# State-space stage: separate homes for delta times x, a first convolution on VectorE, and Softplus in one ScalarE operation

## What is computed

```python
xc, z = jnp.split(layernorm(x) @ W_in.T, 2, axis=-1)
xc = jax.nn.silu(causal_depthwise_conv(xc, conv_w) + conv_b)      # 4 taps per channel
dBC = xc @ W_x.T                                                  # rank 64, then B and C of 16 each
delta = jax.nn.softplus(dBC[..., :64] @ W_dt.T + b_dt)            # the step size
deltaA = jnp.exp(delta[..., None] * -jnp.exp(A_log))
BX = delta[..., None] * Bm[:, :, None, :] * xc[..., None]
hs = scan(h = deltaA * h + BX)                                    # along the 512 positions
y = jnp.einsum('bldn,bln->bld', hs, Cm) + Dp * xc
x = x + (y * jax.nn.silu(z)) @ W_out.T
```

## Time and profile before

| | us |
|---|---|
| median of 3 runs (range) | 2030.31 (2026.47 to 2031.36) |
| the profiled execution's own time | 2027.92 |
| its span, first to last instruction | 2026.2 |
| first scan (half 0 of batch 0) starts | 87.77 |
| state-space block ends, about | 993 |

### The profile page before, as it was taken

How to read it: one execution, slowest core, us unless ns; L and a number is a source line. 1 busy time by engine, 2 the same in 40 slices (tenths; PEclk the granted TensorE clock), 3 DMA queues, 4 the chain that set the end, 5 groups by cost and what they waited for, 6 DMA issues and landing times. The chain is left out here.

```text
span 2026.2 us, 34133 instructions
## 1 busy us (share of the span) xinstructions
PE 1317.7 (65%) x14100; PEld 627.8 (31%) x14100; DVE 1335.6 (66%) x1625; ACT 914.5 (45%) x1685; POOL 1075.5 (53%) x463
## 2 busy tenths in 40 slices
PE   6175765758485765843488746577767777556876
PEld 3021322223131322220233323244444445443333
DVE  1388889998988889899650023786678658617002
ACT  4267475666657475654222214454445434113220
POOL 0488999989898999989600011331452245312000
PEclk9587777869686877866698877787778877678988
DMA  3725537282726547280399950113211222219997
GB/s 93 176 52 148 134 96 185 54 200 53 188 69 154 128 104 167 54 201 28 104 403 421 421 200 14 45 39 67 65 41 46 65 65 44 65 35 389 406 421 282
DMA packets 193707, 300.07 MB, mean 148 GB/s; under 512 B 82704, under 2 KB 125200, under 8 KB 177168
## 3 DMA queue, kind: packets, MB, share of 16 engines
q1 hardware_dynamic: 188512, 295.17, 48.5%
q10 hardware_dynamic: 4688, 2.19, 0.4%
q0 software_dynamic: 352, 0.52, 0.1%
HBM read 255.37 MB, written 42.47 MB: 147 GB/s over the span
## 5 line engine op out<-in xcount | busy, mean ns | idle before, releaser
L369 POOL TENSOR_TENSOR state<-dx_rep,b_rep 128x2048 f32<-128x2048 f32 x128 | 579.0, 4530 | 25.0 <-PE psum L739 24.9
L597 DVE TENSOR_TENSOR_SCAN psum<-psum,state 128x1024 f32<-128x1024 f32 x160 | 365.1, 2282 | 57.3 <-POOL state L369 33.8
L482 ACT ACTIVATE psum<-delta_rep,a_neg 128x511 f32<-128x511 f32 x512 | 331.4, 684 | 68.8 <-DVE state L597 68.7
L739 PE MATMUL psum<-state,sel 128*32 128x512 f32 x1024 | 182.1, 808 | 210.3 <-POOL state L378 209.9
L597 DVE TENSOR_TENSOR_SCAN state<-psum,state 128x1024 f32<-128x1024 f32 x96 | 218.8, 2279 | 37.4 <-ACT psum L482 37.4
L378 POOL TENSOR_TENSOR state<-state,c_rep 128x1024 f32<-128x1024 f32 x96 | 226.4, 2361 | 0.0
L663 PE MATMUL psum<-xt,w_in 128*128 128x512 f32 x256 | 142.7, 709 | 101.2 <-ACT z_silu L441 47.9
L604 DVE TENSOR_TENSOR state<-psum,c_rep 128x1024 f32<-128x1024 f32 x160 | 195.9, 1224 | 5.5
L479 ACT COPY psum<-zeros 128x2 f32<-128x2 f32 x160 | 26.2, 164 | 249.4 <-DVE state L604 241.7
L739 PEld LDWEIGHTS psum<-state,sel 128*32 128x32 f32 x1024 | 27.8, 127 | 334.1 <-issue 314.9
L1852 PE MATMUL psum<-xt_delta,w_qkv 128*128 128x512 f32 x192 | 110.5, 717 | 12.1 <-DVE attn_t L1666 11.3
(11 more groups left out here) (219 smaller groups left out, 2477.4 us busy)
## 6 DMA issues: line engine op xcount, KB each, us to landing
moe_w_set<-in_w SPq DMA_DIRECT2D x30, 4096.0 KB, 33.2
delta_rep<-delta_scratch SPq DMA_DIRECT2D x128, 256.0 KB, 4.7
dx_rep<-dx_scratch SPq DMA_DIRECT2D x128, 256.0 KB, 7.6
b_rep<-bc_scratch SPq DMA_DIRECT2D x32, 256.0 KB, 4.8
delta_scratch<-delta SPq DMA_DIRECT2D x32, 256.0 KB, 5.3
dx_scratch<-delta SPq DMA_DIRECT2D x32, 256.0 KB, 2.0
c_rep<-bc_scratch SPq DMA_DIRECT2D x32, 256.0 KB, 8.1
moe_x<-x_after SPq DMA_DIRECT2D x16, 512.0 KB, 8.8
```

The lines of the kernel that those rows point to most:

```text
L369: nc.gpsimd.tensor_tensor(ring[q % RING][:, :, :], dx_rep[u % CHUNKS][:, :, :], free_bcast(b_rep[q // QPB % 2][:, g, :], 1, CB), ALU.mult) ...
L482: ins = nc.scalar.activation(dec[:, i, 1:], delta_rep[u % CHUNKS][:, c, 1:], ACT.Exp, scale=a_neg[:, dt * CB + c, g:g + 1])
L597: nc.vector.tensor_tensor_scan(bx if by_pool(k) else flat, flat, bx, 0.0, ALU.mult, ALU.add).then_inc(S["scan_done"], 1)
L739: ins = nc.tensor.matmul(bank[32 * c:32 * c + 32, :], sel[:, :], ring[q % RING][:, c, :], start=False, stop=(g == NG4 - 1), skip_group_che ...
```

## The change

- **Softplus.** The four ACT operations and the DVE sum of a block become one `ACT.Softplus` from PSUM into `delta`, which raises `delta_ready` itself. Softplus is in a table set of its own; after each pair of blocks the program asks for the Exp and Ln set again.
- **Homes for dx.** `delta_x` writes elsewhere: for batch 0 into the second `z_silu` buffer, later for blocks 0, 1 into `x_res` and for 2, 3 into `xt`. It no longer waits for the store of delta, but (later batches) for `x_stored` or for `z_psum`; ACT's `xt_copies` now waits for `d_stored` of blocks 2, 3.
- **First convolution.** For batch 0, ACT copies the projection into `xpad` and scales the same PSUM bank by the last tap with the bias; DVE adds the other three taps (three `scalar_tensor_tensor` per block), and ACT's Silu follows. The matmuls and their wait for `conv_diag` go; the making of `conv_diag` (16 operations, L614) moves behind the taps, `dp_diag` and `a_neg`.
- **SP's order for batch 0.** Block by block: store delta, store dx, load the chunk (blocks 0, 1).

```diff
+        def dx_home(b, t):
+            if b == 0:
+                return zs[1][:, t, :]
+            return x_res[:, 2 * t:2 * t + 2, :].rearrange("p s d -> p (s d)") if t < 2 else xt[:, t - 2, :]
...
-                for pair in ((0, 1), (2, 3)):
-                    for t in pair:
-                        store_delta(0, t)
-                    for t in pair:
-                        store_dx(0, t)
-                        if t < 2:
-                            load_chunk(0, t)
-                        if t == 0:
-                            load_replicated(0, 1)
+                for t in range(DT):
+                    store_delta(0, t)
+                    store_dx(0, t)
+                    if t < 2:
+                        load_chunk(0, t)
+                    if t == 0:
+                        load_replicated(0, 1)
...
-                    pool.wait_ge(S[f"d_stored{t}"], 32 * b + 16)
-                    nc.gpsimd.tensor_tensor(delta[:, t, :], delta[:, t, :], xc[b % 2][:, t, :], ALU.mult).then_inc(
+                    if b >= 2 and t < 2:
+                        pool.wait_ge(S["x_stored"], 16 * (b - 1))
+                    if b and t >= 2:
+                        pool.wait_ge(S["z_psum"], DT * (b + 1))
+                    nc.gpsimd.tensor_tensor(dx_home(b, t), delta[:, t, :], xc[b % 2][:, t, :], ALU.mult).then_inc(
...
+                        if b >= 2:
+                            act.wait_ge(S[f"d_stored{2 + kt}"], 32 * b)
                         act.wait_ge(S["xt_psum"], KD * b + kt + 1)
...
+                def first_tap(t):
+                    act.wait_ge(S["xp_psum"], t + 1)
+                    if t >= 2:
+                        act.wait_ge(S["first_conv"], t - 1)
+                    bank = xbank(0, t)
+                    nc.scalar.copy(xpad[t % 2][:, KC - 1:], bank[:, :])
+                    nc.scalar.activation(bank[:, :], bank[:, :], ACT.Identity, bias=conv_b[:, t:t + 1],
+                                         scale=conv_w[:, t, KC - 1:KC]).then_inc(S["xp_read"], 1)
...
-                def softplus_parts(b, pair):
+                def step_sizes(b, pair):
                     for t in pair:
                         act.wait_ge(S["delta_psum"], DT * b + t + 1)
                         if b:
                             act.wait_ge(S[f"d_stored{t}"], 32 * b)
...
+                        nc.scalar.activation(delta[:, t, :], dbank(b, t)[:, :], ACT.Softplus,
+                                             bias=b_dt[:, t:t + 1]).then_inc(S["delta_ready"], 1)
+                    nc.scalar.preload_act_table_set("natural_log_exp_and_others")
...
+                for t in range(DT):
+                    first_tap(t)
                 for t in range(DT):
                     first_silu(t)
-                    if t < 2:
-                        xpad_copy(0, t + 2)
-                nc.scalar.preload_act_table_set("natural_log_exp_and_others")
                 copy_dbc(0)
                 act.wait_ge(S["proj_loaded"], 16 * 3)
-                for t in range(DT):
-                    softplus_parts(0, (t,))
+                step_sizes(0, range(DT))
...
-                def softplus_sum(b, t):
+                def first_taps(t):
+                    for k in range(KC - 1):
+                        if k == 0:
+                            dve.wait_ge(S["xp_read"], t + 1)
+                        else:
+                            dve.wait_ge(S["conv_step"], 2 * t + k)
+                        bank = xbank(0, t)[:, :]
+                        nc.vector.scalar_tensor_tensor(bank if k < KC - 2 else xc[0][:, t, :], xpad[t % 2][:, k:k + L],
+                                                       conv_w[:, t, k:k + 1], bank, ALU.mult, ALU.add).then_inc(
+                            S["conv_step"] if k < KC - 2 else S["first_conv"], 1)
...
-                for t in range(DT):
-                    convolve(0, t)
```

More of the change, by code:

```diff
@@ L223, in mamba_phase @@
             "ln_stats", "ln_mv", "ln_var", "ln_rstd", "ln_shift", "ln_done", "xt_psum", "xt_ready", "xp_psum", "xp_read",
-            "conv_diag", "conv_psum", "conv_done", "xc_ready", "z_psum", "z_read", "dbc_psum", "dbc_ready", "bc_stored",
-            "b_loaded0", "b_loaded1", "c_loaded0", "c_loaded1", "delta_psum", "soft_abs", "soft_exp", "soft_ln", "delta_ready", "dx_ready",
+            "conv_diag", "conv_psum", "conv_done", "conv_step", "first_conv", "xc_ready", "z_psum", "z_read", "dbc_psum", "dbc_ready", "bc_stored",
+            "b_loaded0", "b_loaded1", "c_loaded0", "c_loaded1", "delta_psum", "delta_ready", "dx_ready",
             "d_stored0", "d_stored1", "d_stored2", "d_stored3", "delta_loaded0", "delta_loaded1", "delta_loaded2",
@@ L278, in store_dx @@
                     sp.wait_ge(S["dx_ready"], DT * b + t + 1)
-                    sp.dma_start(dx_dram[b, t * P:(t + 1) * P, :], delta[:, t, :]).then_inc(S[f"d_stored{t}"], 16)
+                    sp.dma_start(dx_dram[b, t * P:(t + 1) * P, :], dx_home(b, t)).then_inc(S[f"d_stored{t}"], 16)
                 def load_chunk(b, t):
@@ L421, in xpad_copy @@
                     if t >= 2:
-                        act.wait_ge(S["conv_psum"], DT * b + t - 1)
+                        act.wait_ge(S["conv_psum"], DT * (b - 1) + t - 1)
                     nc.scalar.copy(xpad[t % 2][:, KC - 1:], xbank(b, t)[:, :]).then_inc(S["xp_read"], 1)
                 def conv_copy(b, t):
-                    act.wait_ge(S["conv_psum"], DT * b + t + 1)
+                    act.wait_ge(S["conv_psum"], DT * (b - 1) + t + 1)
                     nc.scalar.activation(xc[b % 2][:, t, :], xbank(b, t)[:, :], ACT.Identity,
                                          bias=conv_b[:, t:t + 1]).then_inc(S["conv_done"], 1)
+                def first_tap(t):
[6 more added lines that the diff above has]
+                                         scale=conv_w[:, t, KC - 1:KC]).then_inc(S["xp_read"], 1)
                 def first_silu(t):
-                    act.wait_ge(S["conv_psum"], t + 1)
-                    nc.scalar.activation(xc[0][:, t, :], xbank(0, t)[:, :], ACT.Silu, bias=conv_b[:, t:t + 1]).then_inc(
-                        S["xc_ready"], 1)
+                    act.wait_ge(S["first_conv"], t + 1)
+                    nc.scalar.activation(xc[0][:, t, :], xc[0][:, t, :], ACT.Silu).then_inc(S["xc_ready"], 1)
                 def conv_silu(b):
@@ L453, in softplus_parts @@
                             act.wait_ge(S[f"d_stored{t}"], 32 * b)
-                        nc.scalar.activation(delta[:, t, :], dbank(b, t)[:, :], ACT.Relu, bias=b_dt[:, t:t + 1])
-                        nc.scalar.activation(dbank(b, t)[:, :], dbank(b, t)[:, :], ACT.Abs,
-                                             bias=b_dt[:, t:t + 1]).then_inc(S["soft_abs"], 1)
-                    for t in pair:
-                        act.wait_ge(S["soft_abs"], DT * b + t + 1)
-                        nc.scalar.activation(dbank(b, t)[:, :], dbank(b, t)[:, :], ACT.Exp,
-                                             scale=-1.0).then_inc(S["soft_exp"], 1)
-                    for t in pair:
-                        act.wait_ge(S["soft_exp"], DT * b + t + 1)
-                        nc.scalar.activation(dbank(b, t)[:, :], dbank(b, t)[:, :], ACT.Ln,
-                                             bias=1.0).then_inc(S["soft_ln"], 1)
+                        nc.scalar.activation(delta[:, t, :], dbank(b, t)[:, :], ACT.Softplus,
+                                             bias=b_dt[:, t:t + 1]).then_inc(S["delta_ready"], 1)
+                    nc.scalar.preload_act_table_set("natural_log_exp_and_others")
                 def half_decay(k):
@@ L546, in _ @@
                         if i == 22:
[L547 removed]
+                            step_sizes(n, (0, 1))
                         if i == 25:
[L549 removed]
+                            step_sizes(n, (2, 3))
                         if i == 29:
@@ L610, in _ @@
                                         ALU.add).then_inc(S["sel_ready"], 1)
+                dve.wait_ge(S["pads_zero"], 3)
                 dve.wait_ge(S["conv_loaded"], 16 * 2)
+                for t in range(DT):
+                    first_taps(t)
+                dve.wait_ge(S["params_loaded"], 16 * N_PARAMS)
+                for t in range(DT):
+                    nc.vector.tensor_scalar(dp_diag[:, t, :], ident[:, :], dp[:, t:t + 1], None,
+                                            ALU.mult).then_inc(S["dp_diag"], 1)
+                dve.wait_ge(S["a_exp"], NJ)
+                nc.vector.tensor_scalar(a_neg[:, :, :], a_neg[:, :, :], -1.0, None, ALU.mult).then_inc(S["a_ready"], 1)
                 for t in range(DT):
```

25 lines of the change are left out of this document (2 added, 23 removed).

## The result

| | before | after |
|---|---|---|
| median, us (range) | 2030.31 (2026.47 to 2031.36) | 1964.91 (1959.82 to 1966.89) |
| profiled execution, us (its span) | 2027.92 (2026.2) | 1966.89 (1965.2) |

The ratio is 0.9678, with a 95% interval of 0.9651 to 0.9706. 1974 was forecast, with a range of 1956 to 1999. The profiled span fell by 61.0 us.

What follows compares the result with a forecast made beforehand. It took the start's chain and, in the loop, DVE's own work plus late ACT as the bound. Start 30.5 plus loop 26 gave 56.5 us off 2027.92, 1971.4, plus 2.4 for the median: 1974, range 1956 to 1999.

Steps and rivals of the forecast that it cites:

- What bounds the loop: State-space loop: DVE's own work plus places where ACT is late, 60.8 us of DVE waits over 30 waits.
- POOL's waits are slack: Loop: POOL's 42.4 us of waits for delta's stores cost nothing, unless they come back through PE.
- The paragraph on quad 0: Next batch's first quad: POOL starts 3.7 us earlier, DVE 4; late chunks could cost 1 us a batch, 7 in all.
- Start, convolution: Batch 0: taps of 0.75 us from 18.4, cold projection 5.2 from 26.3, `dbc` at 32.1 against 39.91; 1.8 worse at 1.2 GHz.
- Start, chunk: Batch 0, from `dbc` to first scan: chunk 0 called at 41.9, first scan at 57.2 instead of 87.77, gaining 30.5 us.
- Loop, step sizes: End of each batch: half 26 2.4 us earlier, a removed sum 1.2, a shorter wait 0.3; 3.9 a batch, 27 in seven.
- Loop, the norm's shift: DVE's `norm_shift`, now meeting `delta_x` on POOL, would cost up to 0.3 us in six batches.
- the forecast's own case: Whole kernel: start and loop gains as worked out, 1974 us, with its own range 1966 to 1992; chance 0.71.
- All 42.4 us of GpSimd's waits back: Rival, loop: POOL's waits were on the path through PE, so 73 us gained in total, 1957 us; chance 0.12.
- A drain behind each load: Rival, ACT in the loop: each table switch costs 2.57 us, loop gains 0.2 a batch, total 1998 us; chance 0.08.
- The start that stays: Rival, start: DMAs or a cold PE keep the first scan near 85, only the loop gains, 2004 us; chance 0.05.
- Softplus dear: Rival, ACT at i = 25: slower beyond 4.7 us extra a pair; with loads of 5 us, 2069 us; chance 0.04.

Runs made afterwards that it cites:

- softplus_only: Kernel before with only the one-operation Softplus; the product with x still made in place, waiting for delta's store: ratio to before 0.9962, loop 901.3 us.
- homes_only: Kernel before with only the separate homes for dx and SP's new store order; four-part softplus and matmul convolution kept: ratio to before 0.9900.
- homes_softplus: Changed kernel with TensorE's matmul convolution put back for batch 0: ratio to before 0.9779, loop 878.8 us.
- early_dx: Changed kernel with GpSimd's delta_x of blocks 0 and 1 made one quad earlier (after quad 13 instead of 14): ratio to before 0.9845.
- pool_extra: Changed kernel with two more 128x512 products on GpSimd, results unused, ahead of delta_x of blocks 2 and 3 in seven batches: ratio to before 0.9704.
- two_more_loads: Changed kernel with two more table loads on ScalarE behind the step sizes of blocks 2 and 3 in each batch: ratio to before 0.9845.

## Why the prediction came out right, step by step

- **What bounds the loop.** VectorE, with GpSimd behind it: right for the kernel before, and too coarse. "POOL's waits are slack" holds for before by about 0.5 us a batch (estimated above); softplus_only shows them on the path as soon as VectorE is 3.9 faster. The forecast survived because the change brings the homes with it, which the prediction counted for nothing in the loop. The paragraph on quad 0 had this right (GpSimd 3.7 earlier, VectorE 4; up to 7 us back): 3.0 came back, and GpSimd's wait there is 3.0 a batch where the working gave 2.5. VectorE's three waits for GpSimd in the loop, 2.0 us, are one of the prediction's own signs of being wrong, at a small size.
- **Start, convolution.** A tap 0.75 as taken; the scaling copy 0.76, not 0.65. Of `dbc` at 34.42 instead of 32.1, 1.0 is a projection that began at 27.29 instead of 26.3. The first copy came 0.5 later than the 17.09 taken over from before and the scaling took 0.1 more, so the taps began at 19.00 instead of 18.4; the rest is small waits between the engines, and Silu's load followed at 25.22 instead of 24.4. The other 1.3 is the projection at 6.52 instead of 5.2. Its stretch (27.29 to 33.81) had a mean clock of 0.56, so most of it was at 1.2 GHz: near the bad end of the bounds, not the middle row.
- **Start, chunk.** `dbc` to chunk 0's call took 9.78 (9.8 worked out), the call to quad 0 another 11.3 (10.7; the working's own terms, 41.9 + 3.3 + 7.6, add up to 52.8 and not to 52.6), the quad before the scan 4.6. First scan 60.1 against 57.2: 27.6 us, in the range of 26 to 35 and at its low end; 60.1 lies just past the 55 to 60 that was to show it right, by less than the start scatters. That the homes matter most, with SP's order, is shown: 20.4 of it is homes_only and 6.0 comes with the taps; the 1.3 that come with Softplus are within the scatter.
- **Loop, step sizes.** 3.9 us a batch, 27 in 7 was worked out; 27.0 measured, and 22.5 from half 23 to half 30 in each of the seven batches. Half 26's wait went to 1.03 as written.
- **Loop, the norm's shift.** "Up to 0.3 in six batches" was no bound. It held (0.14 each) by luck: in after the shift began 0.1 us before a product of GpSimd ended; homes_softplus met 1.32 and 1.34 in two batches, early_dx 15.04.
- **Not in the prediction:** TensorE's clock at half 11, worth 3.4 in the loop's favour in this pair of traces, which is luck. So the 27.9 that came of the loop, against 26, is 27.0 - 3.0 + 3.4 and 0.4 in 11 to 23.
- **The sum.** 56.5 forecast, 55.5 measured. The median came out 9 us lower than forecast for other reasons: 5.5 is the rest of the span, which scatters; the profiled execution of after lay 2.0 over its median where that of before had lain 2.4 under it, 4.4; less the 1.0. So 1964.91 lies 1 us below the range of the forecast's own case, 1966 to 1992, and within the wider range only, though the two stages together are 1.0 from their forecast.
- **Rivals.** All 42.4 us of GpSimd's waits back: no. The median doesn't tell, since it lies 9 under the forecast and 8 over this rival's 1957; the stages do. 27.0 of the loop's 27.9 stand in 23 to 30, and softplus_only, in which GpSimd waits as before, has the same 157.6 there; pool_extra lengthens GpSimd's work by 2.5 a batch at no price. A drain behind each load: no, 1.29 a load. The start that stays: no. Softplus dear: no, 0.6 each from start to start, 0.69 a row.

## What to carry to other kernels

An engine's waits are slack only up to its distance from the engine that sets the pace: work out that distance before counting a gain on the faster one, since it also caps the gain. Two edits that gained nothing and 3.5 us alone in the loop gained 26 us together, so test the parts and also the pairs. Compare stages, not totals: two_more_loads and early_dx moved in total for reasons (TensorE's clock, one small operation that waits) other than the edit under test.

## What the runs showed of the hardware that I had not expected

- A VectorE operation on four elements a partition, with two tensor inputs in SBUF, took 0.14, 1.35, 3.16 or 15.05 us, by what GpSimd was doing. The waits of 1.35 and 3.16 ended with the GpSimd operation that was running; that of 15.05 in early_dx outlasted five in a row and ended with the sixth, after which GpSimd waited. Four operations with one tensor input, at the same places, took 0.19 to 0.21 each. The Trainium skill, SBUF — State Buffer (Who interferes with whom), says that an operation of VectorE with two SBUF inputs contends with a GpSimd operation that reads SBUF. The runs agree with it on which operations wait. Of operations in a 2-port mode the same section says that whoever issues first has the ports for the whole instruction. The waits of 1.35 and 3.16 are of that length; 15.05 is more than three times the longest GpSimd operation in the block (4.6).
- A store of 256 KB issued behind the loads of a chunk, at 302.15 in softplus_only, landed 8.2 us later, where one without loads ahead landed in 2.0. GpSimd's wait for it was 6.07 us, as in the kernel before (6.05), though delta was ready earlier.
- The same eight matmuls took 3.67 or 5.37 us from batch to batch of one kernel, and up to 6.72 in others (early_dx, at 450.90, with a mean clock of 0.54), and edits that don't touch TensorE moved the sum of the halves 9 to 11 by up to 11 us over the loop.
